# Masked 3x3 convolution of 32 images: five products per row pair in three bands, four in the fourth, and the low part scaled in its PSUM bank

## The reference

```python
m = x.reshape(B, C, 7, 8, 7, 8).mean(axis=(3, 5)) >= 0.05        # per block, repeated to 56 x 56
x_high, x_low = where(m, x, 1e-5), where(m, 1e-5, x)
quant_act(x, s, n)  = clip(round(x / s), 0, n) * s               # n = 255 high, 15 low
quant_w(w, n)       = clip(round(w / t), -n, n) * t, t = max|w| / n   # per output channel, n = 127 high, 7 low
y = conv3x3(quant_act(x_high, ...), quant_w(w_high, ...)) + conv3x3(quant_act(x_low, ...), quant_w(w_low, ...))
```

## Time and profile before

| | |
|---|---|
| median of three runs | 687.96 us |
| span of the profiled execution | 685.9 us |
| TensorE matmul busy | 647.6 us (94%), 3312 instructions |
| VectorE busy | 663.5 us (97%), 902 |
| ScalarE busy | 550.4 us (80%), 616 |
| GpSimd busy | 301.3 us (44%), 240 |
| DMA | 104.07 MB, mean 152 GB/s |

### The profile page before, as it was taken

The page is one execution under the profiler, slowest core; times in us unless marked ns, Lnnn a source line. Parts: engine busy times, 40 slices in busy tenths (PEclk is TensorE's granted clock), DMA queues, the critical chain, the costliest instruction groups (busy, mean ns, idle before and its releaser), DMA issues.

```text
span 685.9 us, 11103 instructions
## 1 busy us (share of the span) xinstructions
PE 647.6 (94%) x3312; PEld 315.9 (46%) x3312; DVE 663.5 (97%) x902; ACT 550.4 (80%) x616; POOL 301.3 (44%) x240
## 2 busy tenths in 40 slices
PE   0489999999999999999999999999999999999998
PEld 0234444444444444444444444444444444444443
DVE  6999999999999999999999999999999999999984
ACT  5588898888898888888888889888889888888843
POOL 5943433553443554353454343355334345434343
PEclk9999999999999999999999999999999999999999
DMA  6222244533344443334443334443333444333223
GB/s 256 94 96 107 122 189 187 187 147 129 125 161 187 187 165 141 122 134 187 187 187 146 115 123 179 187 187 150 136 127 148 187 187 176 141 111 134 95 95 148
DMA packets 14842, 104.07 MB, mean 152 GB/s; under 512 B 1904, under 2 KB 2160, under 8 KB 10864
## 3 DMA queue, kind: packets, MB, share of 16 engines
q1 hardware_dynamic: 14832, 103.95, 39.6%
HBM read 52.56 MB, written 51.38 MB: 152 GB/s over the span
## 4 chain that ended last, share of the span: by engine, by line
PE 85%; DVE 6%; ACT 4%; issue 3%; DMA 1%; DVEq 0%; SPq 0%
PE psum L440 85%; DVE ybuf L678 3%; ACT parts L550 3%; ACT rounded_h L463 1%; DMA act_scale_l<-act_scale_low 1%; DVE pooled L588 0%; DVE chosen L598 0%; DVE v_h L224 0%; DVE clipped_l L604 0%; ACT rounded_l L463 0%; DVE w_max_h L576 0%; DVE plane_h L613 0%; DVE w_max_l L576 0%; ACT wint_l L500 0%; ACT mask_l L481 0%
## 5 line engine op out<-in xcount | busy, mean ns | idle before, releaser
L234 POOL TENSOR_TENSOR sums<-parts 128x448 f32<-128x448 f32 x126 | 140.6, 1136 | 364.4 <-DVE ybuf L678 364.4
L440 PE MATMUL psum<-v_h,wT_h 128*128 128x448 f16 x768 | 192.4, 358 | 9.4 <-DVE ybuf L678 9.3
L440 PE MATMUL psum<-v_l,wT_l 128*128 128x448 f16 x768 | 192.1, 358 | 1.1 <-POOL v_l L228 1.1
L440 PE MATMUL psum<-plane_h,wT_h 128*128 128x448 f16 x864 | 184.4, 358 | 0.0
L440 PE MATMUL psum<-plane_l,wT_l 128*128 128x448 f16 x864 | 182.8, 356 | 0.0
L588 DVE TENSOR_REDUCE pooled<-xbuf 128x7 f32<-128x448 f32 (+1 forms) x213 | 134.6, 632 | 0.0
L238 POOL TENSOR_TENSOR ybuf<-parts,sums 128x896 f32<-128x896 f32 x63 | 131.9, 2094 | 4.9
L678 DVE SCALAR_TENSOR_TENSOR parts<-psum,out_scale_l,parts 128x448 f32<-128x448 f32 x192 | 129.2, 674 | 3.3 <-ACT parts L550 3.2
L440 PEld LDWEIGHTS psum<-plane_h,wT_h 128*128 128x128 f16 x864 | 83.2, 97 | 85.7 <-DVE parts L678 6.3
L440 PEld LDWEIGHTS psum<-plane_l,wT_l 128*128 128x128 f16 x864 | 83.5, 97 | 84.2 <-issue 0.4
L440 PEld LDWEIGHTS psum<-v_h,wT_h 128*128 128x128 f16 x768 | 71.6, 97 | 93.4 <-DVE ybuf L678 23.2
(11 more groups left out here) (73 smaller groups left out, 360.4 us busy)
## 6 DMA issues: line engine op xcount, KB each, us to landing
xbuf<-x SPq DMA_DIRECT2D x31, 1568.0 KB, 7.5
y<-ybuf SPq DMA_DIRECT2D x31, 896.0 KB, 3.9
y<-ybuf SPq DMA_DIRECT2D x32, 672.0 KB, 3.0
xbuf<-x SPq DMA_DIRECT2D x1, 896.0 KB, 8.4
xbuf<-x SPq DMA_DIRECT2D x1, 672.0 KB, 9.6
wraw_h<-w_high SPq DMA_DIRECT2D x1, 576.0 KB, 5.7
wraw_l<-w_low SPq DMA_DIRECT2D x1, 576.0 KB, 6.7
y<-ybuf SPq DMA_DIRECT2D x2, 224.0 KB, 2.7
```

What stands on the lines that cost most here:

```text
L234: ops.tensor_tensor(sums[w][:, e, :], parts[w][:, PART_AT[1], :], parts[w][:, PART_AT[2], :], op).then_inc(summed, 1)
L440: last = nc.tensor.matmul(psum[:, 2 * pair + (k == "l"), 0:N], stationary(k, j, t), moving(k, p, row, j, t), start=(t == 0), stop=(t == co ...
```

## The change

The image is now cut into four bands of 14 output rows, that is 7 pairs of rows; a moving operand is 7 rows x 56 = 392 columns. With the plane rows d0 to d3 that a pair of output rows reads, and the taps g0, g1, g2 of one column:

- In bands 0 to 2 the middle product T = (d1 + d2) * g1 is made once for both rows of the pair, and A = T + d0*g0 + d2*(g2 - g1), B = T + d1*(g0 - g1) + d3*g2. T has a bank of its own; A and B are the rest in two further banks. This is five products of three matmuls each (`PRODUCTS`), for low and for high: 30 matmuls per band.
- Band 3 (`FAST`) is made by the four products M0 to M3, 24 matmuls (in image 0 it is made like the others). Its sums are made by VectorE out of PSUM in four instructions (`fast_rows`).
- The row sums d1 + d2 of the whole image (`row_sums`) and the differences for band 3 (`differences`) are VectorE's. `v03`, `v1`, `v2`, the `parts` and GpSimd's merging are gone; GpSimd has work at the start only.
- Low and high share their banks. TensorE puts low's products in the three (band 3: four) banks of a band, ScalarE multiplies them in place by the ratio of the scales (`low_scaled`), and TensorE adds high's products on top. So there are two sets of four banks, and for each pair of bands TensorE goes low, low, high, high. The finished T is scaled to SBUF by ScalarE with the bias (`shared_tile`), and VectorE adds A and B to it in one instruction per output row of the pair (`out_row`).
- Clipping of high moves from ScalarE (L471) to VectorE and is done together with the shift; the rounded high part is int16 instead of uint8. Pooling is two instructions per image instead of seven. All steps from rounding to the planes are in two parts (32 and 24 rows).
- Image 0 begins as soon as its first 32 rows are prepared; the low weights are loaded first, and both weights are now rounded on VectorE.
- `pool`, `choose` and `clip` are done one image ahead in place of two. Stores are two halves of 28 rows.

```diff
-    BANDS = (("direct", 16), ("winograd", 0), ("direct", 40), ("winograd", 24), ("direct", 48))
+    PAIRS = H // 2
+    BANDS = 4
+    T_ROWS = PAIRS // BANDS
+    N = T_ROWS * W
+    CUT = (0, 4, BY)
+    FAST = (3,)
+        PRODUCTS = {"T": ((None, 3),), "A": ((0, 0), (2, G21)), "B": ((1, G01), (3, 6)),
+                    "M1": ((None, GP),), "M2": (("d1-d2", GM),), "M0": (("d0-d2", 0),), "M3": (("d1-d3", 6),)}
...
+            def low(n, p, band):
+                g = BANDS * n + band
...
+                if new:
+                    pe.wait_ge(s_shared, g - 1)
+                products("l", p, band, "T")
+                if new:
+                    pe.wait_ge(s_out, 2 * g - 3)
+                products("l", p, band, "A")
+                if new:
+                    pe.wait_ge(s_out, 2 * g - 2)
+                products("l", p, band, "B").then_inc(s_low, 1)
+            def high(n, p, band):
...
+                pe.wait_ge(s_scaled, g + 1)
...
+                for tile in "TAB":
+                    products("h", p, band, tile).then_inc(s_high, 1)
...
+                        low(n, p, 2 * pair)
+                        low(n, p, 2 * pair + 1)
+                    high(n, p, 2 * pair)
+                    high(n, p, 2 * pair + 1)
...
+            def low_scaled(n, band):
...
+                act.wait_ge(s_low, g + 1)
+                banks = psum[:, 4 * (band % 2):4 * (band % 2) + tiles, 0:N]
+                nc.scalar.activation(banks, banks, ACT.Identity, scale=ratio[:, 0:1]).then_inc(s_scaled, 1)
...
+                low_scaled(n, 1)
+                shared_tile(n, 0)
+                if after:
+                    quantise("h", *ahead, 0)
+                shared_tile(n, 1)
...
+                    quantise("h", *ahead, 1)
+                low_scaled(n, 2)
+                if after:
+                    act.wait_ge(s_chosen, n + 3)
+                    masks(n + 1, 0, BY)
+                low_scaled(n, 3)
+                shared_tile(n, 2)
+                shared_tile(n, 3)
```

More of the change, by code:

```diff
@@ L84, in conv_program @@
         mask = {k: sb(f"mask_{k}", [P, BY, W], F16) for k in "hl"}
-        parts = [sb(f"parts{w}", [P, 4, N], F32) for w in range(NW)]
-        sums = [sb(f"sums{w}", [P, 2, N], F32) for w in range(NW)]
-        PART_AT = (0, 2, 3, 1)
+        shared = [sb(f"shared{s}", [P, N], F32) for s in range(2)]
+        upper = sb("upper", [P, N], F32)
+        lower = sb("lower", [P, N], F32)
+        outer_taps = {k: sb(f"outer_taps_{k}", [P, 3, C], F16) for k in "hl"}
+        half_taps = {k: sb(f"half_taps_{k}", [P, 3, C], F16) for k in "hl"}
+        neg_out_scale = sb("neg_out_scale", [P, 1], F32)
         wraw = {k: sb(f"wraw_{k}", [P, TAPS, C], F32) for k in "hl"}
@@ L154, in moving, with rows @@
[L154 to L166, removed]
+        def rows(buf, at, stride, count):
+            flat = buf[:, :]
+            return bass.AP(flat.tensor, flat.offset + at, [list(flat.ap[0]), [stride, count], [1, W]])
@@ new lines, in store, with step @@
+                sp.dma_start(yd[bass.ds(n, 1), :, part * half:(part + 1) * half].rearrange("b c n -> (b c) n"),
+                             ybuf[p][:, part * half:(part + 1) * half]).then_inc(s_stored[p], 16)
+            load_after(0, 0)
+            def step(i, p, load=True):
+                store(i, p, 0)
+                if load:
+                    load_after(i + p, 1 - p)
+                store(i, p, 1)
+            step(0, 0)
+            step(0, 1)
+            with sp.Fori(1, B // 2 - 2) as i:
@@ L413, in sum_weights, with products @@
                 last.then_inc(s_w_sum[k], 1)
-            turn_weights("h")
-            turn_weights("l")
-            sum_weights("h")
-            sum_weights("l")
+            def products(k, p, band, tile):
+                out = psum[:, BANK[band % 2][tile], 0:N]
+                parts = [(row, mat + dx, dx) for row, mat in PRODUCTS[tile] for dx in range(3)]
+                for j, (row, mat, dx) in enumerate(parts):
+                    last = nc.tensor.matmul(out, wT[k][:, mat, :], moving(k, p, band, row, dx),
+                                            start=(k == "l" and j == 0), stop=(j == len(parts) - 1),
+                                            skip_group_check=True)
+                return last
@@ L420, in body @@
+            pe.wait_ge(s_wq["l"], 3)
+            turn_weights("l", 0)
+            turn_weights("l", 1)
             def body(i, p, _):
                 n = 2 * i + p
[L422 to L442 removed]
@@ new lines, in _ @@
+            act_scales()
+            weights("l")
+            pool_part(0, 0, 0)
+            choose(0, *PART[0], 1)
+            clip("l", 0, 0)
+            apply_mask("l", 0, 0, 0)
+            row_sums("l", 0, 0, 0)
+            weights("h")
+            clip("h", 0, 0)
+            apply_mask("h", 0, 0, 0)
+            row_sums("h", 0, 0, 0)
+            low_ratio()
+            pool_part(0, 0, 1)
+            choose(0, *PART[1], 2)
+            for k in "lh":
+                clip(k, 0, 1)
@@ new lines, in body @@
+                if not early(n):
+                    dve.wait_ge(s_stored[p], 32 * i)
+                out_row(n, p, 0, 0)
+                out_row(n, p, 0, 1)
+                if after:
+                    clip("h", m, 0)
+                if first_image(n):
+                    for k in "lh":
+                        fast_weights(k)
+                out_row(n, p, 1, 0)
+                out_row(n, p, 1, 1)
+                if after:
+                    apply_mask("l", m, mp, 0)
+                    clip("h", m, 1)
+                    apply_mask("l", m, mp, 1)
+                    row_sums("l", m, mp, 0)
+                    apply_mask("h", m, mp, 0)
+                    row_sums("l", m, mp, 1)
+                    differences("l", m, mp)
```

703 lines of the change are left out of this document (347 added, 356 removed).

## The result

| | before | after |
|---|---|---|
| median | 687.87 us (687.72 to 687.98) | 711.00 us (710.60 to 711.22) |
| ratio | | 1.0336, 95% interval [1.0322, 1.0351] |
| span of the profiled execution | 685.9 us | 709.0 us |
| time per image in the loop | 20.33 us | 21.11 us |

A forecast was written before the change was run, and what follows sets the result against it. A ring of waits, 20.9 us per image against TensorE's 19.7, was to bound. Start 37, one step of 21.4 and 30 of 20.9 give 685.4; the end of 14.8 gives span 700.2, median 702 us, range 685 to 719.

The forecast's parts named there:

- the rival that they come closer to the pure column count: TensorE's matmuls have an overhead of 0.0025 us instead of 0.007, ring 20.45, time 688 us; chance 0.13.
- The ring: Circle of waits, low band 2's last matmul through ScalarE, VectorE and TensorE to the next image's: 20.9 us; chance 0.70.
- Drain: Ring step from band 2's last low matmul until ScalarE starts its scaling: 0.2 us.
- Scaling of three banks in place: Ring step on ScalarE, one instruction over three PSUM banks of 392 columns: 1.22 us, bounds 1.1 to 2.2.
- the rival of taking turns (2.2): ScalarE's in-place scaling alternates reading and writing, 2.2 us; the ring grows by 1.0, time 733 us; chance 0.07.
- mask and hop: Ring step: ScalarE makes the low mask, 0.61 us, then 0.1 until VectorE starts.
- TensorE's 57 matmuls: Ring step: rest of low band 1, high bands 0 and 1, low band 2: 9.88 us.
- VectorE's run: Ring step from the first mask product to the end of band 3's first output row: 8.93 us.
- TensorE's waits in front of A of bands 0 and 1: TensorE idles per image about 0.4 us ahead of A of band 0 and about 0.8 ahead of A of band 1.
- Start and end: Band 2 of image 0 starts at 37 us, uncertain by 3; after band 2 of image 31 come 14.8 us.
- far from 15: Sign of a wrong forecast: the first low matmul starting far from 15 us.
- The rival on the other side: The ring does not bind, being 1.2 us shorter; TensorE's 19.7 sets the pace, about 665 us; chance 0.10.

The follow-up runs named there:

- experiment 1: The kernel after, with the next image's masks made on ScalarE ahead of the scaling of low band 2 instead of behind it: 670.29 us, ratio 0.9737.
- experiment 9: The kernel of experiment 1, with the loads of the two activation scales issued first on SyncE's queue instead of on ScalarE's: 665.32 us, ratio 0.9669.
- experiment 8: The kernel of experiment 1, with an unused VectorE reduction of 1624 elements per image added in front of the first mask product: 679.54 us, ratio 0.9880.
- experiment 3: The kernel after, with VectorE's low differences moved from ahead of band 2's output rows to behind band 3's: 693.98 us, ratio 1.0077.
- experiment 5: The kernel after, with an unused VectorE reduction of 812 elements per image added in front of band 2's output rows: 739.60 us, ratio 1.0749.
- experiment 2: The kernel after, with the next image's masks made one step later, behind the scaling of low band 3: 798.11 us, ratio 1.1612.
- experiment 10: The kernel of experiment 9, with image 0's scaling of low band 0 put ahead of image 1's first rounding on ScalarE: 667.10 us, ratio 0.9694.
- experiment 4: The kernel after, with an unused VectorE reduction of 1624 elements per image added in front of the first mask product: 712.33 us, ratio 1.0355.

## Why the prediction was right

**TensorE.** Right. The forecast counted 114 matmuls at 0.170 and 0.174, 19.7 us; experiment 1, where TensorE alone sets the pace, has 19.69. Twelve wide matmuls take 2.09 us, 0.174 each, and three dense ones 0.51. The rival that they come closer to the pure column count is out. The Trainium skill (TensorE: Matmul & The Clock Gate, back-to-back issue gap) would have 392 / 2.4 + 2.5 ns = 0.166; neither kind agrees, the wide one least. The page gives this for a matmul by itself and says that in a stream it comes out too high for many columns; here it comes out too low.

**The ring, step by step.** Drain 0.20, as forecast. Scaling of three banks in place 1.22, mean 1215 ns in 97 of them: as forecast, and the rival of taking turns (2.2) is out. The Trainium skill's 172 cycles (VectorE: DVE Perf Modes, the TRN2 errata) had given an estimate of 1.12, and the trace doesn't agree. The measured time is the one worked out from rows that write to SBUF, so no gain from writing to PSUM shows. From the start of the scaling to the start of the mask 1.14 pass, and mask and hop are 0.73 for 0.71. TensorE's 57 matmuls 9.88 for 9.88. VectorE's run from the first product to the end of the output row of band 3 is 9.10 (360.96 to 370.06) for 8.93: many steps, read from rows of other sizes, and together 0.17 short. This is the term that was mis-sized, where the forecast called its rows measured within 0.05. The ring is 21.11 and not 20.9, which is 30 x 0.21 = 6.3 us of the 9 by which the forecast is off, and 5.1 of that are this run's.

**The waits.** TensorE's waits in front of A of bands 0 and 1, 0.55 and 0.85 us from start to start, and VectorE's 2.7 in front of L593 are where the forecast put them, at 0.4, 0.8 and 3.

**That these make a ring.** Shown from several sides: moved masks cut it (19.69) or stretch it (23.46, and 23.89 with the clock's share); work taken out of the run shortens it (20.47), work put in lengthens it by the full amount (22.02), and twice as much beside the run does nothing.

The chain of waits of the kernel after (start, us, what) tells it otherwise:

```profile
349.01 14.71 PE psum L317 x84
363.72 0.04 issue
363.76 0.05 DVEq L592
363.81 1.05 DVE plane_h L593
```

It goes from TensorE straight to a `plane_h` product, without the scaling and the mask. VectorE had no idle time there. L592 waits until high's products of an earlier image are counted, which was so long before; the end of high band 2 is a later event of the same semaphore, and it seems that the view took it for the releaser. Only moving the mask showed which way round is real.

**Start and end.** The end was 15.0 for 14.8. The start was 39.7 for 37, within its 3, but by a step that was wrong. The forecast put the first low matmul at 15 us and named "far from 15" as a sign that it is wrong; it came at 19.35. It let VectorE begin on the low weights at 7.4, when the change had moved the loads of the scales to ScalarE's queue, where they land later: VectorE began its first instruction at 9.37 instead of 5.98, and is 3.4 us late from there. The other 1.0 is ScalarE's: the turned weights are ready at 16.45, and their copies start at 17.45, behind the masks of the first part. Of these 4.35 us late, 2.7 were left at band 2, because later steps had been counted too long; that the start stayed within its 3 is partly luck. With the scales on SyncE's queue the start is 37.16 (experiment 9), and the first low matmul comes at 15.95.

**The rival on the other side.** It decided at a ring 1.2 us shorter. One of its reasons was misreckoned: it has VectorE's total 2.6 us under TensorE's, but 17.7 is 2.0 under 19.7 (2.6 is the distance to the 20.3 of the kernel before). In experiment 8, where VectorE is never idle for long, its stream is 20.10 less the 1.75 of the reduction, 18.35 us, so it is 1.3 under. With the masks moved, in experiment 1, the period fell by 1.42 to TensorE's own: 30 x 1.42 = 43 us, less 3 for a later start (40.96) and a longer first step (22.70, with the clock at the lower level for part of it, as in experiment 3); the spans differ by 39.6. So the rival's regime is real, 1.4 us away, and the kernel was not in it.

## What to carry to other kernels

Where every engine has one stream in order, sum up each ring of waits (instruction to instruction, through every engine, back to where it began one iteration later) and compare it with the fullest engine. An engine that is 84% busy can bound through what stands between two of its instructions. Then look for the small instruction that closes the ring (here a mask of 0.6 us that waited behind a scaling that it doesn't need) before removing work: moving it was worth 41 us, and the saving of six matmuls was worth 32 us or less than nothing depending on it.

## What the runs showed of the hardware

- Idleness of 1.3 and 0.7 us on TensorE in each image left the granted clock at 1.00 (experiment 5, over four images). Idleness of 0.6 and then 2.0 us in each image was followed by 12 matmuls at 0.59 (experiment 2), though the first time that it came, at 73 to 76 us, they ran at 1.00 and took 2.1.
- One wait of 2.0 us in image 0 was followed by 12 matmuls in 3.6 to 3.7 us in experiments 1, 3, 5, 9 and 10 (granted clock 0.53 in experiment 3), and in 2.08 us at 1.00 in experiment 4. So the same idleness may or may not cost the upper level; what decides it no run here shows.
- A load of 0.5 KB took 8.2 us from its issue on ScalarE's queue, beside SyncE's large loads, and 4.7 when it was issued on SyncE's, ahead of them. Which of the two counts, the queue or the place ahead of the large loads, no run separates. The Trainium skill (DMA: Bandwidth & Descriptors, issuing engines are not separate DMA queues) says that transfers share the 16 DMA engines whoever issues them; the trace fits that, as a queue of its own did not keep the small load out of the large ones' way.
- ScalarE scaled three PSUM banks in place in 1.22 us and four in 1.53 (mean of 97 and of 31), 0.81 ns per element, the same as between the roundings of 1344 and 1792 elements from SBUF to SBUF.
- `choose` took 1.27 us beside GpSimd's merge and 0.19 with GpSimd idle.
